# A transformer block with routed experts: fixed regions per expert, routing by pairs of batches, tiles through an address table

## The reference

```python
mod = (silu(c) @ wmod).reshape(16, 6, 1, -1)        # sa, ca, ga, sb, cb, gb per batch
h = layernorm(x) * (1 + ca) + sa
x = x + ga * attention(h)        # 16 heads of 8, rotary, causal, softmax
h = layernorm(x) * (1 + cb) + sb
x = x + gb * moe(h)
# moe: 8 experts, top 2 by softmax(h @ router.T), the two shares renormalised;
# y = sum_k share_k * (gelu(h @ w_fc[e_k] + b_fc[e_k]) @ w_proj[e_k] + b_proj[e_k])
```

## Time and profile before

| | us |
|---|---|
| median of three runs | 740.84 |
| lowest, highest | 733.06, 742.04 |
| the profiled execution | 746.82 |
| its span | 745.1 |
| PE matmuls busy in the span | 531.1 (71%) |
| DVE busy | 425.8 (57%) |
| POOL busy | 336.4 (45%) |
| ACT busy | 307.8 (41%) |

### The profile page before, as it was taken

One profiled execution on the slowest core, in us unless ns is written; L12 is line 12 of the kernel. 1 busy time (PEld: TensorE's weight loads), 2 busy tenths in 40 slices (PEclk: granted clock), 3 DMA queues, 4 the chain that ended last, 5 costly groups with the idle time before them and its releaser, 6 DMA issues.

```text
span 745.1 us, 13855 instructions
## 1 busy us (share of the span) xinstructions
PE 531.1 (71%) x3976; PEld 413.6 (56%) x3976; DVE 425.8 (57%) x1180; ACT 307.8 (41%) x859; POOL 336.4 (45%) x438
## 2 busy tenths in 40 slices
PE   0547777743787787788767775868776666899960
PEld 0325555532555565566545543547776666899950
DVE  3545677451567766776696754624573333467753
ACT  0003444221344443444442522535673444677740
POOL 7112244130234334424434767761646556456552
PEclk9768999776898998999898987967998889999985
DMA  3023556899331133123303314101112222133433
GB/s 97 25 71 103 117 174 204 164 130 133 95 102 57 46 102 101 37 66 102 95 16 100 90 58 125 49 29 29 48 43 65 52 57 57 51 83 111 128 98 115
DMA packets 77498, 63.77 MB, mean 86 GB/s; under 512 B 9810, under 2 KB 71771, under 8 KB 77328
## 3 DMA queue, kind: packets, MB, share of 16 engines
q1 hardware_dynamic: 71888, 54.27, 31.2%
q0 software_dynamic: 4544, 8.47, 3.4%
q10 hardware_dynamic: 1024, 0.53, 0.3%
HBM read 25.40 MB, written 16.69 MB: 56 GB/s over the span
## 4 chain that ended last, share of the span: by engine, by line
PE 35%; DVE 22%; issue 15%; SPq 11%; DMA 7%; ACT 4%; another core or an unknown queue 2%; POOL 2%; DVEq 1%; POOLq 0%; ACTq 0%
PE ps_sc L1288 7%; DVE maxima L1146 5%; SPq L454 5%; PE ps_pv L1417 4%; PE ps_pv L1295 3%; PE ps_max L1295 3%; DVE z L929 3%; PE ps_sc L1386 2%; PE ps_sc L1390 2%; PE misc L1432 2%; PE misc L1462 2%; ACT after_k L747 2%; PE ps_max L1365 2%; DMA k_diags<-k_stack 2%
## 5 line engine op out<-in xcount | busy, mean ns | idle before, releaser
L782 ACT ACTIVATE probs<-ps_sc 128x512 f32<-128x512 f32 x192 | 114.2, 597 | 265.0 <-PE ps_sc L1386 161.9
L1146 DVE TENSOR_REDUCE maxima<-ps_max 128x2 f32<-128x512 f32 (+1 forms) x192 | 131.5, 686 | 138.0 <-PE ps_max L1367 90.0
L650 POOL TENSOR_SCALAR_AFFINE_SELECT probs<-probs 128x512 f32<-128x512 f32 x128 | 83.6, 660 | 116.9 <-ACT probs L782 115.9
L618 POOL DMA_INDIRECT results<-after_k x78 | 79.4, 1018 | 87.0 <-DVE after_k L945 66.8
L1288 PE MATMUL ps_sc<-x_in,after_k 128*128 128x128 f32 x624 | 92.4, 295 | 27.3 <-ACT x_in L753 14.0
L1288 PEld LDWEIGHTS ps_sc<-x_in,after_k 128*128 128x128 f32 x624 | 82.2, 205 | 32.4 <-issue 16.4
L747 ACT ACTIVATE after_k<-ps_sc,after_k 128x128 f32<-128x128 f32 x312 | 98.6, 374 | 1.2 <-PE ps_sc L1288 0.9
L1386 PE MATMUL ps_sc<-q_stacks,k_diags 128*128 128x256 f32 x256 | 71.7, 367 | 27.7 <-DMA q_stacks<-shift_t 27.7
L1417 PE MATMUL ps_pv<-probs,v_wides 128*32 128x256 f32 (+1 forms) x1024 | 66.5, 386 | 21.3 <-POOL probs L650 17.3
L609 POOL DMA_INDIRECT sorted_rows<-rows,slots x64 | 64.1, 1001 | 18.1 <-issue 16.6
L1386 PEld LDWEIGHTS ps_sc<-q_stacks,k_diags 128*128 128x128 f32 x256 | 46.8, 223 | 30.0 <-DMA q_stacks<-shift_t 19.6
(11 more groups left out here) (149 smaller groups left out, 970.9 us busy)
## 6 DMA issues: line engine op xcount, KB each, us to landing
k_diags<-k_stack SPq DMA_DIRECT2D x64, 128.0 KB
sorted_rows<-blank_s SPq DMA_DIRECT2D x1, 5070.0 KB, 51.2
after_k<-sorted_rows SPq DMA_DIRECT2D x78, 65.0 KB
k_stack<-high SPq DMA_DIRECT2D x32, 128.0 KB, 2.1
q_stacks<-high SPq DMA_DIRECT2D x32, 128.0 KB
gate_now<-gate_rows SPq DMA_DIRECT2D x16, 256.0 KB
x_in<-in_x SPq DMA_DIRECT2D x16, 128.0 KB, 2.3
k_stack<-low SPq DMA_DIRECT2D x16, 128.0 KB, 2.1
```

The source lines that it names most:

```text
L618: nc.gpsimd.indirect_dma_start(result_dram, bass.IndirectOffsetOnAxis(ap=row_in[u][:, D + 1:D + 2].bitcast(U32), axis=0), y_out[u], None, ...
L650: nc.gpsimd.affine_select(four, four, [[0, 4], [1, P]], ALU.is_ge, 0.0, base=0, channel_multiplier=-1).then_inc(S["causal_done"], 1)
L782: nc.scalar.activation(probs[:, g % 2, c], ps_sc[u % 2][:], ACT.Exp, scale=SCALE).then_inc(S["exp_done"], 1)
L1146: nc.vector.tensor_reduce(to, of, AX, ALU.max).then_inc(S["max_done"], 1)
```

## The change

- The loop over steps 4 to 11 is written out; `Step.value`, `hold` and `pick` go, all waits are against constants.
- Groups are batches 0 to 11 and 12 to 15, so 55 and 23 tiles, 78 as before. In the sorted buffer every expert has a region of fixed size (`CAP`, 25 and 9 tiles), and 7 blank tiles lie at the end. So a token's slot is the expert's running base plus its rank, and routing goes by pairs of batches: pair p in step 4 + 2p, each operation in a slot of its own; its rows are sorted in the next step (`SORT_AT`) and in slots 0 and 2 of the one after.
- Only the blank tiles are cleared (7 of 128 rows instead of 78), in step 13. The end of each region is padded by one indirect DMA per expert (`pad`, 8 a group).
- `list_step` works out, in 12 small operations of DVE on one partition, each tile's expert (`expert_of`) and its place (`tile_at`): for group 0 in step 15 and slots 0 and 1 of step 16. SP reads `tile_at` into a register for every row load.
- w_fc and w_proj are loaded one expert a step (two DMAs of 256 KB) in steps 4 to 11, the biases in step 12.
- Tiles start in step 16 at slot 8 (`first_tile` in slot 7) instead of step 17 at slot 3, so 16 of them are placed in steps 16 and 17 instead of 9; in each slot an engine does the step's own work first, then the tile's.
- Beside the tiles, pair 6 is sorted behind tiles 6 to 16 and pair 7 behind tiles 29 to 39 (two of three tiles, one DMA each), pads behind tiles 27, 28 and 40 to 47. Pair 7 is routed beside tiles 17 to 26, its list beside 26 to 31.
- Twelve batches are finished in the last three rounds (four a round) and four behind the last tile.
- The turned rows use one PSUM bank instead of two, and `ps_y` takes its two banks in the other order.

```diff
-FIRST, LAST = 4, 12
-GROUP_B = (LAST - 2, B - (LAST - 2))
+GROUP_B = (12, B - 12)
+CAP = [n + 1 for n in GROUP_TILES]
+REGION = [0, EXPERTS * CAP[0]]
+BLANK_AT = REGION[1] + EXPERTS * CAP[1]
-TILES_AT = 3
+TILES_AT = 8
+def tile_of_slot(t, n):
+    return (t - B) * UNITS + n - TILES_AT
-SORT_PARTS = (0, 4, 6, 12, 16, 18, 24, 28, 30, 36, 38, 40, 40, 40, 40, 40)
+SORT_AT = {2: (0, 0), 4: (0, 1), 6: (0, 2), 8: (0, 3), 10: (1, 0), 11: (1, 1)}
+SORT_LATER_AT = {0: (1, 2), 2: (1, 3)}
+PAD_AT = {1: 0, 3: 1, 5: 2, 7: 3, 9: 4}
+PAD_LATER_AT = {1: 5, 3: 6, 4: 7}
 def steps(eng, emit):
-    for t in range(-2, FIRST):
-        emit(Step(t))
-    with eng.Fori(0, (LAST - FIRST) // 2) as i:
-        for u in range(2):
-            emit(Step(FIRST + u, i, u))
-    for t in range(LAST, B + 2):
+    for t in range(-2, B + 2):
         emit(Step(t))
...
-                    sp.dma_start(sorted_dram.rearrange("(p t) r -> p t r", p=P),
+                    sp.dma_start(sorted_dram[BLANK_AT * P:].rearrange("(p t) r -> p t r", p=P),
...
             def load_row(i, u):
+                at = sp.value_load(entry(tile_at, i, u), min_val=0, max_val=SORTED_TILES - 1)
...
+            sp.wait_ge(S["listed"], 1)
+            sp.wait_ge(S["blank_out"], 16)
+            sp.wait_ge(S["padded_a"], 16 * EXPERTS)
             sp.wait_ge(S["sorted_a"], 16 * 2 * GROUP_TILES[0])
-            sp.wait_ge(S["score_mm"], UNITS * B)
-            sp.wait_ge(S["pv_mm"], 4 * B)
...
+            def place(s):
...
+                wide = [P, FOUR + 1, EXPERTS]
+                bank = misc[BANK["router"]]
+                nc.vector.tensor_tensor(slot_all[:], bank[:, RANKS_AT:RANKS_AT + (FOUR + 1) * EXPERTS].rearrange("p (n e) -> p n e", e=EXPERTS),
+                                        base[:].rearrange("p (o e) -> p o e", o=1).broadcast_to(wide), ALU.add).then_inc(S["ranked"], 1)
+            def move_base(s):
+                s.pair_wait(dve, S["ranked"], 0, 1, 1)
+                nc.vector.tensor_copy(base[:], slot_all[:, FOUR]).then_inc(S["based"], 1)
...
+                    m = tile_of_slot(s.t, n)
+                    if m == -1:
+                        first_tile()
+                    elif m >= 0:
+                        tile(*round_of(m))
...
-                    if u in (3, 5):
-                        final(PAIR * (i - FIRST_ROUNDS - 1) + u // 5)
+                    if u % 3 != 2:
+                        final(4 * (i - FIRST_ROUNDS - 1) + 2 * (u // 3) + u % 3)
```

More of the change, by code:

```diff
@@ L114, in pick @@
[L114 to L131, removed]
@@ L134, in steps, with routes, sorts, pair_wait @@
-def steps(eng, emit):
-    for t in range(-2, FIRST):
-        emit(Step(t))
-    with eng.Fori(0, (LAST - FIRST) // 2) as i:
-        for u in range(2):
-            emit(Step(FIRST + u, i, u))
-    for t in range(LAST, B + 2):
+        eng.wait_ge(sems[b % 2], 16 * (b // 2 + 1))
+    def routes(self):
+        return self.t % 2 == 0 and 0 <= self.pair < PAIRS
+    def sorts(self):
+        return self.t % 2 == 1 and 0 <= self.pair < PAIRS
+    def pair_wait(self, eng, sem, back, per, n):
+        if self.pair - back >= 0:
+            eng.wait_ge(sem, (self.pair - back) * per + n)
@@ L142, in steps @@
+def steps(emit):
+    for t in range(-2, B + 2):
         emit(Step(t))
@@ L305, in block_program @@
         row_scaled = sb("row_scaled", [P, TILES, D])
[L306 to L316, removed]
+        rows = sb("rows", [P, 2 * FOUR, ROW])
@@ new lines, in block_program @@
+        slot_f = sb("slot_f", [P, FOUR, 2])
+        slots = sb("slots", [P, FOUR, 2], U32)
+        row_of = sb("row_of", [P, 1])
+        pad_slots = sb("pad_slots", [P, 2, EXPERTS], U32)
+        taken = sb("taken", [1, EXPERTS])
+        over = sb("over", [1, EXPERTS, GROUP_TILES[0]])
+        tiles_of = sb("tiles_of", [1, EXPERTS])
+        ahead = sb("ahead", [1, EXPERTS, EXPERTS])
+        starts = sb("starts", [1, EXPERTS + 1])
+        jump_base = sb("jump_base", [1, 2, EXPERTS])
+        jumps = sb("jumps", [1, 2, EXPERTS + 1])
@@ L606, in sort_rows @@
-            def sort_rows(group, k, tiles, signal):
-                for n in tiles:
-                    nc.gpsimd.indirect_dma_start(
-                        sorted_dram, bass.IndirectOffsetOnAxis(ap=slots[:, k, n:n + 1], axis=0),
-                        rows[:, n, :], None).then_inc(S[signal], 16)
+            for g in range(2):
+                nc.gpsimd.memset(jump_base[:, g, 0:EXPERTS - 1], float(CAP[g])).then_inc(S["consts_in"], 1)
+                nc.gpsimd.memset(jump_base[:, g, EXPERTS - 1:EXPERTS],
+                                 float(BLANK_AT - REGION[g] - (EXPERTS - 1) * CAP[g])).then_inc(S["consts_in"], 1)
+                nc.gpsimd.memset(jumps[:, g, 0:1], float(REGION[g])).then_inc(S["consts_in"], 1)
@@ L726, in _ @@
                     send(i, u)
[L727 to L731 removed]
+                    if u % 3 != 2:
+                        final(4 * (i - FIRST_ROUNDS - 1) + 2 * (u // 3) + u % 3)
+            for b in range(GROUP_B[0], B):
                 final(b)
@@ new lines, in keep_slots, with find_pads @@
+            def keep_slots(s):
+                s.pair_wait(dve, S["slot_f_done"], 0, 1, 1)
+                if s.pair <= GROUP_PAIRS[0]:
+                    s.pair_wait(dve, S["sorted_a"], 1, 16 * 2 * FOUR, 16 * 2 * FOUR)
+                else:
+                    dve.wait_ge(S["sorted_b"], 16 * 2 * FOUR * (s.pair - GROUP_PAIRS[0]))
+                nc.vector.tensor_copy(slots[:], slot_f[:]).then_inc(S["slots_done"], 1)
+            def find_pads(group):
+                dve.wait_ge(S["based"], sum(GROUP_PAIRS[0:group + 1]))
+                nc.vector.tensor_scalar(pad_slots[:, group], base[:], row_of[:, 0:1], None, ALU.add).then_inc(S["pads_ready"], 1)
```

682 lines of the change are left out of this document (380 added, 302 removed).

## The result

The changed kernel takes 681.5 us (median of 4 runs, 678.4 to 683.6) where the kernel before takes 741.4: a ratio of 0.922, 95% interval 0.913 to 0.931. The forecast was 681. The total is right, and much of what it was summed from is not. The trace tells which parts.

What follows compares the result with a forecast made beforehand. In even steps neither PE (81% busy) nor DVE (71%) was full, DVE's maxima waiting for PE. Terms summing to -62.7 us took the profiled 746.8 to 684, and 681 for the median; range 657 to 713.

Steps and rivals of the forecast that it cites:

- A: Clearing 7 tiles of the sorted buffer instead of 78 removes the slow step t = 4: -29 us.
- B: Expert weights loaded in eighths in steps 4 to 11: 0 us, as -4 early and +4 later.
- C: Steps 4 to 11 written out, without register waits, counters and dynamic indices: -4 us, from -8 to +12.
- D: Bursts of group 0's routing and sorting leave their steps, with part of the mask waits: -23 us.
- E: Routing and sorting six pairs in the steps before the tiles adds DVE and POOL work: +19 us, +8 to +31.
- Rival 2: Pairs cost full length, POOL's DMAs delay masks, weight loads cost, written-out steps give nothing: 703 us, chance 0.12.
- F: First tile starts in step 16, slot 7, before the last product with v: -6 us, from -8 to +3.
- rival 4: Chain of last sorting, pads, list, row loads and weight stagings runs past slot 7: 694 us, chance 0.08.
- G: Expert tiles take 193.4 us instead of 210.6, with 0.55 per scatter beside them: -17 us, -35 to +2.
- rival 1: Tiles don't gain: unnamed waits follow the number of POOL's DMAs, or final sums bind DVE; 698 us, chance 0.15.
- H: After the tiles, four batches are left instead of six, at 1.4 us each: -2.7 us.

Runs made afterwards that it cites:

- the written-out kernel: The kernel before with only steps 4 to 11 written out, nothing else changed: 726.2 us beside 744.8, ratio 0.978.
- the extra scatters: The changed kernel with eight more POOL scatters into a spare buffer in tiles 48 to 59: 697.6 us with 128 rows each, 696.1 with 32.
- the plain stores: The changed kernel with eight plain 65 KB DMAs into a spare buffer in tiles 48 to 59: 679.0 us from POOL's queue, 679.6 from SP's.

## Why the prediction was right, and where only its sum was

- **A, clearing, -29.** Right in kind: the slow step is gone. Its size is 25.5 in the written-out kernel (49.3 less 23.84), and 10 to 13 when put back into the changed one.
- **B, 0.** Right in sum; neither half of it was found.
- **C, written-out steps, -4.** The step that failed first: "I find no more than 0.5 us a step between them". It is -14.5 in steps 4 to 11 and about -16 in all, outside the bound. I compared looped steps with written-out ones that carried other work, and took DVE's idle time to have one place, the maxima; 2.1 us of two steps stood open elsewhere in the trace.
- **D, bursts, -23.** Right, and shown from the other side by the bursts put back: 2.7 us for one of four DMAs. Of the 14.1 us that I took for mask waits, 3.9 had no releaser in the profile.
- **E, pairs, +19.** Too dear. A clean step of the written-out kernel takes 23.84 us and steps 10 and 11 of the changed one 24.56 and 24.50: 1.4 a pair with its share of the weights, where I had 2.9 and 1 for the weights. (That is from two clean steps; by the mean of steps 4 to 11, 25.2 and 26.1 in the two traces, against the 24.4 of steps 5 to 11 there, it is 1.6 and 3.3.) DVE's operations overlap one another (78 ns more busy time for each in the kernel that issues them twice), and POOL's DMAs, one to a slot, are in these figures too. Rival 2 was the wrong way round.
- **F, earlier start, -6.** The stretch from step 15 gained 6.5, where with the masks' waits and the list I had 8.7. The chain is POOL's, as rival 4 had it in part, with the eight pads in it.
- **G, tiles, -17.** The other step that failed: "I take 0.55" for a scatter beside tiles, halfway to nothing because POOL would keep up. POOL does keep up. The cost is 1.2 to 1.3 each all the same, and does not come from its time; 24 times the difference is some 16 us. Quieter parts gave some of it back, so that -7.8 is left. My rival 1 named this cause, the number of POOL's DMAs and not their density, and the row against my value was on the table. I took the lower figure because I could price POOL's queue and could not price a wait without a name.
- **H, end, -2.7.** Measured -2.4.

The two misses have opposite signs and nearly cancel; that the median came out at the forecast is luck.

The rule that I weighed against G (the Trainium skill, SBUF — State Buffer, "SBUF: two separate sides") has a DMA of POOL wait for DVE's copies, 620 ns becoming 3,100. Here the extra scatters, placed among the staging copies, take 962 ns on POOL:

```profile
L756 POOL DMA_INDIRECT spare_rows<-rows,places_s x7 | 6.7, 962 | 2.1 <-issue 2.1
```

One of them has copies beside it for 798 of its 966 ns; five have none and take 959 to 963. So the measurement is against the rule, as the mean of 1,001 ns was for the sorting DMAs. It is of the time on POOL alone, and the plain stores met no copy and say nothing. The scatters beside tiles were dear for another reason, which that rule doesn't name.

## What to carry to other kernels

Price a wait whose releaser the profile can't name by counting what it comes with, and don't explain it away by a resource that isn't full. A scatter of POOL right behind another one costs a tight pipeline some 1.2 us, with 32 rows as with 128, while a plain transfer or POOL's computing in the same place is nearly free: write blanks with plain DMAs in small pieces ahead of time, and leave the scatters where engines have slack. And before a loop is taken for free, add up an engine's idle time at its waits on itself in a looped step, against the same instructions in straight code.

## What the runs showed of the hardware

- PE's semaphore increments come out late, several at once, while scatters of POOL follow sends: up to 3.5 us after the instruction's end beside the extra ones and up to 6.2 in the kernel before, each borne out by ACT's start; with plain DMAs in their place ACT starts after 0.04 us. I had not expected an engine's increments to be held up by another's DMA.
- A scatter of 32 rows costs no less than one of 128 (1.7 and 1.3 us), though its instruction on POOL is a little shorter (866 and 962 ns).
- Broadcast clears of 5 MB cost 10 to 30 us in one piece on SP's queue and nothing that shows in twelve.
- Spells at half clock (1.2 GHz) come in every trace, at other places each time. One of 10 to 14 us in step 2 or 3 made that step 2 to 7 us longer in eight of the ten traces with late weights and in none of the four with early ones; in the changed kernel's trace PE was 79% busy at full clock in the step before it. Whether the weights' place does it is open.
